# Two context attentions of 16 heads: TensorE's cycle in the order turned scores, weighted sums, scores, values, keys

## The chip, the cores and the metric

The kernel runs on one core of a Trainium2 chip. The metric is the device time of one execution in microseconds (us); lower is better. The engines are TensorE (PE in the rows; PEld is its weight load), VectorE (DVE), ScalarE (ACT), GpSimd (POOL) and the queue that issues transfers (SP).

## The reference, cut to what matters

The program is a perceiver of twelve sublayers on a residual `x` of 16 x 64 tokens of width 256, with a context of 16 x 1601 rows of width 128. Two of its sublayers, L1_xattn and L3_xattn, are context attentions with 16 heads of 16 numbers each. For each of the 16 batches and each head they compute

```
q = ln(x) @ Wq            # 64 queries
k = context @ Wk          # 1601 keys
v = context @ Wv          # 1601 values
o = softmax(q @ k.T * 0.25) @ v
x = x + o @ Wo
```

L1_xattn has biases on top of that, L3_xattn has none. All numbers are 32-bit floats. Nothing else of the program is touched by the change.

## The kernel before, in words

Both sublayers call `head_attention` (line 2740 on), the only function that changes. It walks through 16 batches of 7 units, each unit being two tiles of 128 keys (the seventh is one tile of 65). Line 2774 makes one loop of cycles `t` from -13 to 117, and every engine runs through it with its own share of the work. In cycle `t` TensorE does, for different units in a software pipeline:

- **turned scores** of unit t (`scores_turned`): four matmuls that put minus the row maximum into four PSUM banks (L2942), then 16 groups of four matmuls of keys against queries on top (L2951). ScalarE takes the exponentials of the four banks (`exps`, L3019).
- **values** of unit t+10 (`values`, L2915): one bank; VectorE copies it (`values_out`, L3095 in L3_xattn, L3098 with a bias in L1_xattn).
- **keys** of unit t+12 (`keys`, L2905): one bank; ScalarE copies it (`keys_out`, L3028).
- once a batch, **turn** (`max_turned`, L2981): the row maxima of the next batch are transposed, and VectorE makes minus_max of them (`shift_rows`, L3083).
- once a batch, **spread** (`sums_spread`, L2987): the sums of the exponentials; ScalarE copies them (L3039), VectorE inverts them and scales the output (`normal_out`, L3103 and L3105).
- in L1_xattn, in four cycles of seven, **context** (`context`, L2895): transposes of context rows into one bank, which ScalarE copies (L3047).
- **scores** of unit t+8 (`scores`, L2930): eight matmuls into four banks, from which VectorE takes maxima, one instruction for each bank (`block_max`, L3070), and after the last unit of a batch the row maximum (`row_max`, L3077).
- **weighted sums** of unit t-1 (`weighted`, L2971): 64 matmuls of exponentials against values, all into bank 7.

Below, T, V, K, C, S and W stand for turned scores, values, keys, context, scores and weighted sums. A cycle has a type, `t mod 7`: in type 5 the scores are those of the 65-key unit and the spread runs, in type 6 the turned scores are short and the turn runs, in type 0 the weighted sums are short, in type 1 the keys, in type 3 the values. Context runs in types 1 to 4 (short in type 4).

What ties the order of the work to time is the ring of PSUM banks. All fills but the weighted sums take banks 0 to 6 in turn, in TensorE's order. A fill may begin only when the fill seven places before it has been read out by its engine; `plan` (line 2803, and the loop from 2807 on) lists the fills in TensorE's order, and `wait_bank` sets the wait:

```python
if place[fill] >= banks:            # banks = 7
    by, count = taken[place[fill] - banks]
    pe.wait_ge(by.sem, by.at(count))
```

Both `scores` and `scores_turned` wait for all four of their banks before their first matmul. The order of VectorE's loop (line 3110 on) was values_out, shift_rows, block_max and row_max, normal_out; that of ScalarE's loop is exps, keys_out, sums_out, context_out, weighted_out.

Of the kernel before, what the change touches and what calls it, by code (L numbers as in the profile page):

```python
# [2739 lines left out]
def head_attention(core, room, Q, made, wv, biased, wo, wo_rows, oT, scale):  # L2740
# [16 lines left out]
    heads, d, groups = 16, 16, 4  # L2757
# [21 lines left out]
    def unit(t):  # L2779

        return divmod(t, turns) if 0 <= t < total else None

    def at_batch(t, after):

        b, rest = divmod(t - after, turns)
        return b if rest == 0 and 0 <= b < BATCH else None
# [16 lines left out]
    def plan(fill, by, count):  # L2803
        place[fill] = len(taken)
        taken.append((by, count))

    for t in cycles:
        if unit(t) is not None:
            for i in range(groups):
                plan(("turned", t, i), exp_done, 4 * t + i + 1)  # L2810
        due = []
        if unit(t + v_lead) is not None:
            due.append(("values", t + v_lead))
        if unit(t + k_lead) is not None:
            due.append(("keys", t + k_lead))
        if (b := at_batch(t, turn_at)) is not None:
            due.append(("turn", b))
        if (b := at_batch(t, spread_at)) is not None:
            due.append(("spread", b))
        if (n := context_part(t)) is not None:  # L2820
            due.append(("context", n))
        for fill in due:
            fill_no[fill] = len(fill_no)
            count, by = (dve_no, side_dve) if fill[0] in ("values", "turn") else (act_no, side_act)
            count[fill] = len(count)
            plan(fill, by, count[fill] + 1)
        if unit(t + s_lead) is not None:
            for i in range(groups):
                plan(("scores", t + s_lead, i), max_done, 4 * (t + s_lead) + i + 1)

    def bank_of(*fill):
        return place[fill] % banks
# [7 lines left out]
    with ExitStack() as own:  # L2840
# [11 lines left out]
        with nc.Block() as block:  # L2852
# [29 lines left out]
            def _(pe):  # L2882
# [36 lines left out]
                def scores(t):  # L2919
                    b, u = divmod(t + s_lead, turns)  # L2920
                    lo, cols, chunks = key_cuts(u)

                    made = act_no["keys", b * turns + u]
                    pe.wait_ge(side_act.sem, side_act.at(made + 1))
                    for i in range(groups):
                        wait_bank(pe, "scores", t + s_lead, i)
                    for n, c in enumerate(chunks):
                        for i in range(groups):
                            rows = slice(32 * i, 32 * i + 32)
                            last = nc.tensor.matmul(PS[:, bank_of("scores", t + s_lead, i), n * cols:(n + 1) * cols], Q[rows, c, b, :],  # L2930
                                                    kT[rows, b % 2, c, lo:lo + cols], start=True, stop=True)
                    last.then_inc(s_ready.sem, 1)
# [45 lines left out]
                def max_turned(b):  # L2978
                    pe.wait_ge(top_ready.sem, top_ready.at(b + 1))
                    wait_bank(pe, "turn", b)  # L2980
                    nc.tensor.transpose(PS[:, bank_of("turn", b), 0:P], M[:].rearrange("p i s -> p (i s)"),  # L2981
                                        core.ident[:]).then_inc(side_ready.sem, 1)
# [8 lines left out]
                for t in cycles:  # L2991
                    if unit(t) is not None:
                        scores_turned(t)
                    if unit(t + v_lead) is not None:
                        values(t + v_lead)
                    if unit(t + k_lead) is not None:
                        keys(t + k_lead)
                    if (b := at_batch(t, turn_at)) is not None:
                        max_turned(b)
                    if (b := at_batch(t, spread_at)) is not None:  # L3000
                        sums_spread(b)
                    if (n := context_part(t)) is not None:
                        context(n)
                    if unit(t + s_lead) is not None:
                        scores(t)
                    if unit(t - 1) is not None:
                        weighted(t - 1, 0)
                        weighted(t - 1, 1)

            @block.scalar  # L3010
            def _(act):
# [50 lines left out]
            @block.vector  # L3062
            def _(dve):
                def block_max(t):
                    b, u = divmod(t + s_lead, turns)
                    lo, cols, chunks = key_cuts(u)
                    dve.wait_ge(s_ready.sem, s_ready.at(t + s_lead + 1))
                    for i in range(groups):
                        bank = PS[:, bank_of("scores", t + s_lead, i), 0:len(chunks) * cols].rearrange("p (c s) -> p c s", s=cols)
                        nc.vector.tensor_reduce(part[:, b % 2, chunks[0]:chunks[-1] + 1, i, u // 2], bank, AX_X,  # L3070
                                                ALU.max).then_inc(max_done.sem, 1)

                def row_max(b):
                    dve.wait_ge(max_done.sem, max_done.at((b + 1) * turns * 4))
                    if b:
                        dve.wait_ge(side_ready.sem, side_ready.at(fill_no["turn", b - 1] + 1))
                    nc.vector.tensor_reduce(M[:].rearrange("p i s -> p s i")[:, 0:DC, :], part[:, b % 2], AX_X,  # L3077
                                            ALU.max).then_inc(top_ready.sem, 1)

                def shift_rows(b):  # L3080
                    dve.wait_ge(side_ready.sem, side_ready.at(fill_no["turn", b] + 1))
                    for c in range(DC):
                        last = nc.vector.tensor_scalar(shift[:, b % 2, c, :], PS[:, bank_of("turn", b), 0:P], pair_sel[:, c:c + 1], None,  # L3083
                                                       ALU.mult).then_inc(m_ready.sem, 1)
                    dve.wait_ge(m_ready.sem, m_ready.at(2 * b + 2))
                    dve.sem_inc(side_dve.sem, 1)

                def values_out(t):
                    b, j = divmod(t, turns)
                    kk, many = keys_of[2 * j], len(tiles_of(j))  # L3090
                    dve.wait_ge(side_ready.sem, side_ready.at(fill_no["values", t] + 1))
                    bank = PS[0:kk, bank_of("values", t), 0:many * DIM].rearrange("p (k h d) -> p k h d", h=heads, d=d)
                    out = V[0:kk, b % 2, 2 * j:2 * j + many, :, 0:d]
                    if not biased:
                        ins = nc.vector.tensor_copy(out, bank)  # L3095
                    else:
                        add_on = made.bv[0:kk, :].rearrange("p (h d) -> p h d", d=d).unsqueeze(1).broadcast_to([kk, many, heads, d])
                        ins = nc.vector.tensor_tensor(out, bank, add_on, ALU.add)  # L3098
                    ins.then_inc(side_dve.sem, 1)

                def normal_out(b):
                    dve.wait_ge(side_act.sem, side_act.at(act_no["spread", b] + 1))
                    nc.vector.reciprocal(inverse[:, b % 2, :], inverse[:, b % 2, :]).then_inc(inverted.sem, 1)  # L3103
                    dve.wait_ge(inverted.sem, inverted.at(b + 1))
                    nc.vector.tensor_tensor(oT[:, :, b * SEQ:(b + 1) * SEQ], O[:, b % 2, :].rearrange("p (g s) -> p g s", s=SEQ),  # L3105
                                            inverse[:, b % 2, :].rearrange("p (g s) -> p g s", s=SEQ),
                                            ALU.mult).then_inc(norm_done.sem, 1)

                nc.vector.memset(PS[:, out_bank, 0:4 * SEQ], 0.0).then_inc(filled.sem, 1)
                for t in cycles:  # L3110
                    if unit(t + v_lead) is not None:
                        values_out(t + v_lead)
                    if (b := at_batch(t, turn_at)) is not None:
                        shift_rows(b)
                    if unit(t + s_lead) is not None:
                        block_max(t)
                        if (t + s_lead) % turns == turns - 1:
                            row_max((t + s_lead) // turns)
                    if (b := at_batch(t, spread_at)) is not None:
                        normal_out(b)  # L3120
    for s in (exp_done, max_done):
# [1011 lines left out]
```

## Time and profile before

| what | us |
|---|---|
| median of 3 runs | 4622.57 |
| lowest and highest run | 4617.99, 4632.91 |
| the profiled execution's own time | 4627.87 |
| its span | 4626.1 |
| L1_xattn's loop, first to last matmul | 1668.8 to 2313.8 |
| L3_xattn's loop, first to last matmul | 3684.5 to 4288.2 |
| TensorE busy, whole span | 4177.0 (90%) |
| VectorE busy, whole span | 2563.9 (55%) |
| ScalarE busy, whole span | 1782.1 (39%) |

The two loops together are 1249 us of the span. In both, TensorE is busy for some 93 to 97 of 100 us, VectorE for 48 to 66 and ScalarE for 43 to 50. The times to read are starts of groups in the timeline: the distance from the start of one group to the start of the next is what it costs TensorE, since the ends of matmuls are modelled and overlap the next start a little.

### The profile page before, as it was taken

Reading aid. Unit: us, or ns where it says so; the run is one execution under the profiler, and the core shown is the slowest. Engines: PE = TensorE matmul, PEld = TensorE weight load, DVE = VectorE, ACT = ScalarE, POOL = GpSimd, SP = SyncE. Lnnn points to the kernel's source line nnn. Section 1 sums busy time; section 2 is a strip of 40 time slices with the busy share of each in tenths; the row PEclk is TensorE's granted clock in tenths of the full one; section 3 lists DMA queues with packets and bytes.
Section 4 is the critical chain, followed back from the end, with each engine's and each line's share of the span. In section 5 each row is a group of like instructions: output and inputs, shape, how many; then the busy total and the mean of one; then the engine's idle time right before and its main releaser. Section 6 shows DMA issues by size and latency. Waiting matters only on the chain. (4 is left out here: it accounts for less than half of the span.)

```text
span 4626.1 us, 107755 instructions
## 1 busy us (share of the span) xinstructions
PE 4177.0 (90%) x44428; PEld 3167.9 (68%) x44428; DVE 2563.9 (55%) x5138; ACT 1782.1 (39%) x3751; POOL 848.0 (18%) x556
## 2 busy tenths in 40 slices
PE   8989999999888989999976789886899999999987
PEld 5669998999667956666642379752699766666465
DVE  4468777777253055555539832246443466665454
ACT  2245555555222424444534312120254344444221
POOL 1222222221101200000029611006222100000201
PEclk9999999999988999999988899898899999999999
DMA  1010000000104821111012168649111000000100
GB/s 35 27 36 18 17 17 17 17 17 1 49 1 174 306 74 44 45 45 45 17 47 78 46 253 314 247 158 141 51 45 54 22 31 24 24 24 10 39 15 10
DMA packets 137827, 305.05 MB, mean 66 GB/s; under 512 B 51800, under 2 KB 87584, under 8 KB 119744
## 3 DMA queue, kind: packets, MB, share of 16 engines
q1 hardware_dynamic: 132992, 287.01, 19.7%
q0 software_dynamic: 4416, 12.06, 0.8%
q8 instruction: 310, 5.08, 0.5%
q14 instruction: 109, 0.89, 0.1%
HBM read 273.46 MB, written 23.47 MB: 64 GB/s over the span
## 5 line engine op out<-in xcount | busy, mean ns | idle before, releaser
L3070 DVE TENSOR_REDUCE block_max<-PS 128x1 f32<-128x512 f32 (+1 forms) x896 | 505.3, 626 | 300.7 <-PE PS L2930 299.9
L3019 ACT ACTIVATE probs_turned<-PS 128x512 f32<-128x512 f32 (+1 forms) x896 | 434.7, 570 | 562.8 <-PE PS L2951 562.7
L1149 PE MATMUL PS<-context_turned,queries 128*128 128x422 f32 (+2 forms) x1536 | 335.3, 360 | 4.8 <-ACT probs L1218 1.9
L1181 PE MATMUL PS<-probs_turned,context_part 128*128 128x256 f32 (+1 forms) x2496 | 327.7, 285 | 2.2 <-DVE weighted L1260 2.2
L1210 ACT CAST probs_turned<-PS 128x512 fp32r<-128x512 f32 (+1 forms) x512 | 232.4, 511 | 229.2 <-PE PS L1161 229.2
L1226 DVE TENSOR_TENSOR probs_turned<-PS,probs_turned 128x512 fp32r<-128x512 f32 (+1 forms) x512 | 276.5, 581 | 75.0 <-ACT probs_turned L1210 73.1
L1181 PEld LDWEIGHTS PS<-probs_turned,context_part 128*128 128x128 f32 (+1 forms) x2496 | 304.2, 189 | 2.4 <-DVE probs_turned L1226 2.4
L2971 PEld LDWEIGHTS PS<-probs_turned,values 128*17 128x17 f32 x13312 | 191.6, 97 | 150.1 <-issue 123.5
L1149 PEld LDWEIGHTS PS<-context_turned,queries 128*128 128x128 f32 x1536 | 262.5, 191 | 32.9 <-ACT probs L1218 9.0
L1218 ACT ACTIVATE probs<-PS,minus_max 128x844 f32<-128x844 f32 (+1 forms) x256 | 238.6, 932 | 105.1 <-DVE minus_max L1271 103.9
L2930 PE MATMUL PS<-keys_turned,queries 32*128 32x512 f32 (+1 forms) x2048 | 241.4, 548 | 40.9 <-ACT probs_turned L3019 35.9
L1161 PE MATMUL PS<-ident,probs 128*128 128x128 f32 (+1 forms) x1664 | 236.5, 278 | 18.5 <-DVE probs_turned L1226 16.8
L1266 DVE TENSOR_REDUCE row_max<-PS 128x1 f32<-128x844 f32 (+1 forms) x256 | 241.7, 980 | 17.7 <-issue 12.7
L2971 PE MATMUL PS<-probs_turned,values 128*17 128x64 f32 x13312 | 232.5, 220 | 10.8 <-issue 9.9
L2915 PE MATMUL PS<-L_xattn_Wv,context_turned 128*128 128x256 f32 (+1 forms) x832 | 237.3, 404 | 0.0
L134 PE MATMUL PS<-ident 128*128 128x256 f32 x706 | 199.9, 434 | 35.5 <-PEq L3940 6.9
L2951 PEld LDWEIGHTS PS<-queries,keys_turned 32*128 32x128 f32 x6656 | 221.4, 182 | 8.7 <-issue 2.3
L2951 PE MATMUL PS<-queries,keys_turned 32*128 32x128 f32 x6656 | 225.0, 270 | 0.9 <-issue 0.8
L3606 PE MATMUL PS<-prod,ident 128*128 128x512 f32 x256 | 148.9, 720 | 80.9 <-POOL prod L3541 56.4
L1161 PEld LDWEIGHTS PS<-ident,probs 128*128 128x128 f32 (+1 forms) x1664 | 185.5, 140 | 52.0 <-DVE probs_turned L1226 29.9
L2905 PE MATMUL PS<-context_turned,wk 128*128 128x512 f32 (+1 forms) x512 | 216.9, 516 | 4.5 <-POOL values L2879 3.9
L2430 PE MATMUL PS<-slot_turned,routed_up 128*128 128x128 f32 x1472 | 201.0, 278 | 4.5 <-ACT slot_turned L2360 2.6
(542 smaller groups left out, 7507.4 us busy)
## 6 DMA issues: line engine op xcount, KB each, us to landing
context_rows<-in_ctx SPq DMA_DIRECT2D x40, 768.0 KB
context_turned<-ctx_turned SPq DMA_DIRECT2D x32, 800.5 KB
routed_up<-in_L_ffn_W SPq DMA_DIRECT2D x23, 1024.0 KB, 7.9
routed_down<-in_L_ffn_W SPq DMA_DIRECT2D x23, 1024.0 KB, 6.0
routed_up<-in_L_ffn_wg_w SPq DMA_DIRECT2D x23, 1024.0 KB, 7.7
routed_second<-in_L_ffn_w_w SPq DMA_DIRECT2D x23, 1024.0 KB, 10.2
routed_down<-in_L_ffn_w_w SPq DMA_DIRECT2D x23, 1024.0 KB, 5.1
v_all<-v_turned SPq DMA_DIRECT2D x128, 128.0 KB, 17.5
```

What stands on the lines that cost most here:

```text
L1149: last = nc.tensor.matmul(PS[:, j, 0:cols], qs[a][:, v, p * P:(p + 1) * P], yT[b][:, v, at:at + cols], start=(m == 0), stop=(m == 2))
L1161: last = nc.tensor.transpose(PS[0:kk, turn_bank(it, local, j), (k - 4 * j) * P:(k - 4 * j + 1) * P], probs[:, (local - 1) % 2, k * P:k * P ...
L1181: last = nc.tensor.matmul(O_ps, yp[a][0:kk, u, k, :], probsT[b][0:kk, par, k, :], start=(k == 0 and m == 0), stop=(k == KT - 1 and m == 2))
L1218: nc.scalar.activation(out, S[half], ACT.Exp, bias=bias[:, local % 2:local % 2 + 1], scale=scale, accum_out=total[:, local, half:half + 1] ...
L1226: nc.vector.tensor_tensor(rest, bank, lead, ALU.subtract).then_inc(t_dve.sem, 1)
L1266: nc.vector.tensor_reduce(top[:, q, half:half + 1], S[half], over, ALU.max).then_inc(step.sem, 1)
L2915: last = nc.tensor.matmul(PS[0:kk, bank_of("values", t), n * DIM:(n + 1) * DIM], room.y[b % 2][:, kt * P:kt * P + kk], wv[:], start=True, ...
L2930: last = nc.tensor.matmul(PS[:, bank_of("scores", t + s_lead, i), n * cols:(n + 1) * cols], Q[rows, c, b, :], kT[rows, b % 2, c, lo:lo + c ...
L2951: last = nc.tensor.matmul(PS[0:kk, bank_of("turned", t, i), at:at + P], kT[rows, b % 2, c, kt * P:kt * P + kk], Q[rows, c, b, :], start=Fa ...
L2971: last = nc.tensor.matmul(PS[32 * i:32 * i + wide, out_bank, g * SEQ:(g + 1) * SEQ], V[0:kk, b % 2, kt, 8 * a + 4 * c + i, :], probs[0:kk, ...
L3019: nc.scalar.activation(probs[0:kk, t % ring, i, 0:many].rearrange("p k c s -> p (k c s)"), PS[0:kk, bank_of("turned", t, i), 0:many * 2 * ...
L3070: nc.vector.tensor_reduce(part[:, b % 2, chunks[0]:chunks[-1] + 1, i, u // 2], bank, AX_X, ALU.max).then_inc(max_done.sem, 1)
```

## The change

TensorE's cycle becomes T, turn, W, S, V, K, spread, C. Before it was T, V, K, turn, spread, C, S, W. `plan` lists the fills in the new order, so that the bank ring follows it. VectorE's loop becomes shift_rows, block_max and row_max, values_out, normal_out. ScalarE's loop is as before. The numbers of instructions and their shapes are the same; all leads (8, 10, 12, 13 units) are too.

```diff
     for t in cycles:
         if unit(t) is not None:
             for i in range(groups):
                 plan(("turned", t, i), exp_done, 4 * t + i + 1)
+        if (b := at_batch(t, turn_at)) is not None:
+            plan_side(("turn", b))
+        if unit(t + s_lead) is not None:
+            for i in range(groups):
+                plan(("scores", t + s_lead, i), max_done, 4 * (t + s_lead) + i + 1)
         due = []
         if unit(t + v_lead) is not None:
             due.append(("values", t + v_lead))
         if unit(t + k_lead) is not None:
             due.append(("keys", t + k_lead))
-        if (b := at_batch(t, turn_at)) is not None:
-            due.append(("turn", b))
...
-        if unit(t + s_lead) is not None:
-            for i in range(groups):
-                plan(("scores", t + s_lead, i), max_done, 4 * (t + s_lead) + i + 1)
```

```diff
                 for t in cycles:
                     if unit(t) is not None:
                         scores_turned(t)
+                    if (b := at_batch(t, turn_at)) is not None:
+                        max_turned(b)
+                    if unit(t - 1) is not None:
+                        weighted(t - 1, 0)
+                        weighted(t - 1, 1)
+                    if unit(t + s_lead) is not None:
+                        scores(t)
                     if unit(t + v_lead) is not None:
                         values(t + v_lead)
                     if unit(t + k_lead) is not None:
                         keys(t + k_lead)
-                    if (b := at_batch(t, turn_at)) is not None:
-                        max_turned(b)
...
-                    if unit(t + s_lead) is not None:
-                        scores(t)
-                    if unit(t - 1) is not None:
-                        weighted(t - 1, 0)
-                        weighted(t - 1, 1)
```

```diff
                 for t in cycles:
-                    if unit(t + v_lead) is not None:
-                        values_out(t + v_lead)
                     if (b := at_batch(t, turn_at)) is not None:
                         shift_rows(b)
                     if unit(t + s_lead) is not None:
                         block_max(t)
                         if (t + s_lead) % turns == turns - 1:
                             row_max((t + s_lead) // turns)
+                    if unit(t + v_lead) is not None:
+                        values_out(t + v_lead)
```

TensorE in L3_xattn, one whole cycle of type 2 before, from its turned scores (`minus_max`, then `queries,keys_turned`) to the next ones; values are `L_xattn_Wv,context_turned`, keys `context_turned,wk`, scores `keys_turned,queries`, weighted sums `probs_turned,values`:

```order
L2942 MATMUL PS<-minus_max,ones_wide 128x512 x4
L2951 MATMUL PS<-queries,keys_turned 128x128 x16
L2915 MATMUL PS<-L_xattn_Wv,context_turned 128x256 x2
L2905 MATMUL PS<-context_turned,wk 128x512
L2930 MATMUL PS<-keys_turned,queries 128x512 x4
L2971 MATMUL PS<-probs_turned,values 17x64 x32
L2942 MATMUL PS<-minus_max,ones_wide 128x512 x4
```

And the same place after (all line numbers of this function are 3 higher there):

```order
L2945 MATMUL PS<-minus_max,ones_wide 128x512 x4
L2954 MATMUL PS<-queries,keys_turned 128x128 x16
L2974 MATMUL PS<-probs_turned,values 17x64 x32
L2933 MATMUL PS<-keys_turned,queries 128x512 x4
L2918 MATMUL PS<-L_xattn_Wv,context_turned 128x256 x2
L2908 MATMUL PS<-context_turned,wk 128x512
L2945 MATMUL PS<-minus_max,ones_wide 128x512 x4
```

Between the turned scores and the scores stood the values and the keys, now the weighted sums; between the scores and the next turned scores stood the weighted sums, now the values and the keys.

VectorE in L3_xattn around the end of a batch before, from the maxima of the short scores (type 5) to the maxima of the next unit (type 6):

```order
L3070 TENSOR_REDUCE block_max<-PS 128x2 x4
L3077 TENSOR_REDUCE row_max<-block_max 128x2x4
L3103 RECIPROCAL row_scale<-row_scale 128x256
L3105 TENSOR_TENSOR oT<-weighted,row_scale 128x4x64
L3095 COPY values<-PS 128x32x16
L3083 TENSOR_SCALAR minus_max<-PS,pair_sel 128x128 x2
L3070 TENSOR_REDUCE block_max<-PS 128x1 x4
```

And after:

```order
L3073 TENSOR_REDUCE block_max<-PS 128x2 x4
L3080 TENSOR_REDUCE row_max<-block_max 128x2x4
L3098 COPY values<-PS 128x32x16
L3106 RECIPROCAL row_scale<-row_scale 128x256
L3108 TENSOR_TENSOR oT<-weighted,row_scale 128x4x64
L3086 TENSOR_SCALAR minus_max<-PS,pair_sel 128x128 x2
L3073 TENSOR_REDUCE block_max<-PS 128x1 x4
```

A copy of values has moved from between the scaled output and minus_max to ahead of the reciprocal; minus_max now follows the scaled output directly.

## Rows read from the trace of the kernel before

**Rows 1.** The page's section 5: the scores' group, its idle time and releasers.
```profile
L2930 PE MATMUL PS<-keys_turned,queries 32*128 32x512 f32 (+1 forms) x2048 | 241.4, 548 | 40.9 <-ACT probs_turned L3019 35.9
```

**Rows 2.** Timeline, L3_xattn, TensorE: start us, us, engine, line, out<-in xcount [idle before]
```profile
4022.55 0.50 PE L2942 MATMUL PS<-minus_max,ones_wide 32*128 32x512 f32 x4
...
4023.88 1.13 PE L2915 MATMUL PS<-L_xattn_Wv,context_turned 128*128 128x256 f32 x4
4024.84 1.02 PE L2905 MATMUL PS<-context_turned,wk 128*128 128x512 f32 x2
4025.81 1.14 PE L2930 MATMUL PS<-keys_turned,queries 32*128 32x512 f32 x8
4026.88 1.09 PE L2971 MATMUL PS<-probs_turned,values 128*17 128x64 f32 x64
4027.90 0.51 PE L2942 MATMUL PS<-minus_max,ones_wide 32*128 32x512 f32 x4
...
4031.15 1.14 PE L2930 MATMUL PS<-keys_turned,queries 32*128 32x512 f32 x8 [0.42 <-ACT probs_turned L3019]
...
4043.94 0.39 PE L2942 MATMUL PS<-minus_max,ones_wide 32*128 32x256 f32 x4
```

**Rows 3.** Timeline, L3_xattn, a cycle of type 0: TensorE, VectorE and ScalarE.
```profile
4015.19 1.14 PE L2930 MATMUL PS<-keys_turned,queries 32*128 32x512 f32 x8
...
4016.39 2.48 DVE L3070 TENSOR_REDUCE block_max<-PS 128x1 f32<-128x512 f32 x4 [1.27 <-PE PS L2930]
...
4017.23 0.51 PE L2942 MATMUL PS<-minus_max,ones_wide 32*128 32x512 f32 x4 [0.33 <-DVE block_max L3070]
...
4018.75 2.06 ACT L3019 ACTIVATE probs_turned<-PS 128x512 f32<-128x512 f32 x4 [1.41 <-PE PS L2951]
```

**Rows 4.** Timeline, L1_xattn before its first turned scores, TensorE.
```profile
1680.46 1.14 PE L2930 MATMUL PS<-keys_turned,queries 32*128 32x512 f32 x8
...
1683.70 1.14 PE L2930 MATMUL PS<-keys_turned,queries 32*128 32x512 f32 x8 [0.18 <-DVE block_max L3070]
...
1687.53 0.71 PE L2930 MATMUL PS<-keys_turned,queries 32*128 32x512 f32 x4 [0.79 <-DVE block_max L3070]
```

**Rows 5.** Timeline, L1_xattn, one batch, TensorE.
```profile
2017.86 0.39 PE L2942 MATMUL PS<-minus_max,ones_wide 32*128 32x256 f32 x4
...
2028.02 0.51 PE L2942 MATMUL PS<-minus_max,ones_wide 32*128 32x512 f32 x4 [0.33 <-DVE block_max L3070]
...
2031.75 1.14 PE L2930 MATMUL PS<-keys_turned,queries 32*128 32x512 f32 x8 [0.43 <-ACT probs_turned L3019]
...
2056.70 0.39 PE L2942 MATMUL PS<-minus_max,ones_wide 32*128 32x256 f32 x4
2056.92 0.61 PE L2951 MATMUL PS<-queries,keys_turned 32*65 32x128 f32 x16
2057.46 1.13 PE L2915 MATMUL PS<-L_xattn_Wv,context_turned 128*128 128x256 f32 x4
```

**Rows 6.** Timeline, L3_xattn, cycles of type 5 and 6: all engines.
```profile
4003.99 1.02 PE L2905 MATMUL PS<-context_turned,wk 128*128 128x512 f32 x2
...
4004.85 0.59 PE L2987 MATMUL PS<-weighted,sum_spread 128*128 128x256 f32 x2
...
4005.64 0.42 ACT L3039 COPY row_scale<-PS 128x256 f32<-128x256 f32 x1
...
4007.06 0.39 PE L2942 MATMUL PS<-minus_max,ones_wide 32*128 32x256 f32 x4
...
4007.21 1.74 DVE L3103 RECIPROCAL row_scale<-row_scale 128x256 f32<-128x256 f32 x1
...
4008.98 0.42 DVE L3105 TENSOR_TENSOR oT<-weighted,row_scale 128x256 f32<-128x256 f32 x1
...
4009.96 0.61 DVE L3083 TENSOR_SCALAR minus_max<-PS,pair_sel 128x128 fp32r<-128x128 f32 x2
```

**Rows 7.** Busy time by stretch, us and count: PE PEld DVE ACT POOL, granted clock, DMA share, GB/s.
```profile
2200.00:2300.00 100.00, 92.77 (x2223) 64.81 (x2220) 55.70 (x99) 50.38 (x111) 0.00 (x0) 1.00 0.05 19
```

More of the change, by code:

```diff
@@ L2805, in plan, with plan_side @@
         taken.append((by, count))
+    def plan_side(fill):
+        fill_no[fill] = len(fill_no)
+        count, by = (dve_no, side_dve) if fill[0] in ("values", "turn") else (act_no, side_act)
+        count[fill] = len(count)
+        plan(fill, by, count[fill] + 1)
     for t in cycles:
@@ L2822, in head_attention @@
         for fill in due:
[L2823 to L2826, printed above, removed]
-        if unit(t + s_lead) is not None:
-            for i in range(groups):
-                plan(("scores", t + s_lead, i), max_done, 4 * (t + s_lead) + i + 1)
+            plan_side(fill)
     def bank_of(*fill):
```

## The prediction

> **What bounds the kernel now.** I read the page's groups first. Only the two 16-head attentions change, so their groups matter: the scores (S) have TensorE idle for 40.9 us ahead of them over both, 35.9 us of it until ScalarE has read turned scores [rows 1]. That is the wait which this order of work touches, and it is no more than 0.8% of the kernel.
>
> Next comes the timeline of TensorE in the steady part, because only the distances between starts say what a step costs. A full cycle of L3_xattn is T 1.33 (4023.88 - 4022.55), V 0.96, K 0.97, S 1.07, W 1.02, in all 5.35, and none of it is a wait [rows 2]. TensorE is the bound here. In the next cycle V is short and S waits 0.42 for ScalarE: it starts 3.25 after T [rows 2]. The wait is for a bank. The ring has seven banks; with V and K between T and S, the last scores bank is the one that the third turned bank left. With one fill more between (context, in L1_xattn) it is the fourth, and S starts 3.73 after T [rows 5]. So exponentials come free 0.48 apart: fourth 3.73, third 3.25, and by the same step second 2.76 and first 2.27 after T (the last two are estimates from these rows).
>
> VectorE has its own staircase. The maxima start 1.20 after S and take 2.48 for four [rows 3]. Where the next waiting fill needs only the first of them read, it starts 2.04 after S (4017.23 - 4015.19) [rows 3]. Where it needs three, or four, the part of L1_xattn before its first turned scores shows it: there a cycle is S, V, K, and the next S starts 3.24 later, idle 0.18 for block_max; with a context fill between as well it starts 3.83 later, idle 0.79 in spite of the extra work [rows 4]. One step is 0.6, so first 2.04, third 3.24 and fourth 3.83 agree.
>
> **The change, part by part.** No instruction is added or removed. What moves is the distance, in fills and in time, between a bank's fill and its next use.
>
> *The wait of S.* Between T and S now stands W, which takes no bank, so the last scores bank needs only the first exponential read, 2.27 after T. TensorE gets there at 1.33 + 1.02 = 2.35 [rows 2]. The wait is gone in the full cycles, and 0.08 is all the cover that is left. In type 0 W is half as long, TensorE is there at about 1.9, and S starts at 2.27.
>
> *The wait of T.* Before, between S and the next T stood W alone, with no fill, and T needed one maximum: 2.04 after S, where TensorE came at 1.07 + 1.02 = 2.09 (hidden, but in type 0). Now V and K stand between, two fills, and T's fourth bank is the one of the third score: 3.24 after S. TensorE comes at 1.07 + 0.96 + 0.97 = 3.00. So T waits 0.24 in a full cycle, and where V or K is short it waits longer and the short fill gains nothing. Everything behind T on TensorE's queue waits with it. In L1_xattn with context three fills stand between, and T needs all four maxima: 3.83.
>
> So a cycle of types 1 to 4 costs 2.35 + 3.24 = 5.59 in L3_xattn and 2.35 + 3.83 = 6.18 in L1_xattn. Type 0 costs 2.27 + 3.24 = 5.51. Type 5 has the short scores, whose maxima are done early, and the spread: T 1.33, W 1.02, S some 0.60, V 0.96, K 0.86 and spread 0.59 [rows 2, 6], about 5.37, the same work as before with no wait.
>
> *The order on VectorE, type 5 into 6.* Before, the spread ran ahead of the short scores and its reciprocal began right after row_max. Now the spread comes last in the cycle. Count from the start of S in type 5: the next T is at 5.37 - 2.35 = 3.02, the spread at 2.43, K at 1.57; ScalarE's copy starts 1.65 after K (4005.64 - 4003.99) and takes 0.42, so it ends at 3.64; the reciprocal runs from 3.7, the product 1.77 later at 5.47, until 5.89; then minus_max 0.61, to 6.50 [rows 6]. The maxima of the next scores stand behind that. Without it they would start at 3.02 + 0.76 + 0.2 + 1.02 + 1.20 = 6.20 (short T 0.76 [rows 5]; the turn's 0.2 is an estimate, a third of the spread), so they are 0.3 late. The third maximum releases T 3.24 - 1.20 = 2.04 after they begin, at 8.54: type 6 costs 8.54 - 3.02 = 5.52. If nothing were late it would be 5.22.
>
> *The sum of a batch.* L3_xattn: 5.51 + 4 x 5.59 + 5.37 + 5.52 = 38.76, against 4043.94 - 4007.06 = 36.88 [rows 2, 6]: 1.88 more. L1_xattn: 5.51 + 4 x 6.18 + 5.37 + 5.52 = 41.12, against 2056.70 - 2017.86 = 38.84 [rows 5]: 2.28 more. K runs out at t = 99 of 112, so cycles 1 to 98 are 14 full batches: 26.3 and 31.9, together **58.2 us**.
>
> *Edges.* Before the first turned scores the order S, V, K is the old one turned round, with the same waits; the first S comes one V and K earlier (-1.9), and the first T waits for three maxima in place of one (+1.2): -0.7 in each stage. The first batch has no reciprocal (-0.3 each). In the last cycles V or K is missing, and what a shorter wait of S gives, T's wait takes back: 0, between -1 and +1. In all about -2.
>
> *What costs nothing.* W needs exponentials of the cycle before, a cycle old now as then. weighted_out (ScalarE, behind keys_out) ends some 0.2 before the next W wants bank 7. Copies of values start 3.7 after S and end by 4.5, a microsecond before the next S needs their bank. SP's transfers of context hang on V, K or context of a batch, each later by under a cycle, with more than ten cycles to land in. ScalarE's order is unchanged and it is busy half the time [rows 7].
>
> The sum is +56. On the profiled execution's 4627.87 that is 4684; that one is 5.3 above the median of the three runs, so for the median I take 4622.6 + 56 = **4679 us**.
>
> **A rule against the order, weighed.** In a stretch of L1_xattn in which TensorE waited about as often as it will now, it was busy for 92.77 of 100 us and the granted clock stayed 1.00, the 2.4 GHz level [rows 7]. The Trainium skill, Perfetto Trace Analysis, section Matmul Optimizations, says that TensorE's power follows its use, so that matmuls should run back to back. By that rule a gap in every cycle could cost clock on top of the gap. By rows 7 the sum has no term for it; the rule's result is the third rival.
>
> **The rivals.**
>
> *Faster: the wait of T is not there.* VectorE would have to finish three maxima in 3.00 after S rather than 3.24; the point is a maximum of 0.52 rather than 0.60. Then only the gain is left, at most all of the 35.9 us for which S waited on ScalarE [rows 1]: 4587. For it speaks that the gap is only 0.24, under a tenth of a microsecond per instruction. Against it speaks that rows 4 show this very wait, behind the same V and K. 4 in 100.
>
> *A smaller cost.* If T in a context cycle had only to wait for three maxima, TensorE's own work would set it, at some 5.8 rather than 6.18: 0.4 x 56 cycles = 22 less, 4657; a reciprocal that delays nobody gives 0.3 x 26 = 8 less, 4671. The fourth bank follows from counting fills, and rows 4 show 3.83. 6 in 100 for the first.
>
> *The clock falls.* If one twentieth of the two stages (1249 us in all) ran at 1.2 GHz, the same work would take double there: about +60, 4739. 3 in 100, since rows 7 show no such fall.
>
> *S waits for a later exponential.* The cover is 0.08. If the first exponential came 0.1 to 0.18 later after T than I take it, each of 140 cycles (types 1 to 5, 14 batches, both stages) would lose 0.02 to 0.1: 3 to 14 more, up to 4693, inside my range. If it were the second (2.76), each would lose 0.4 and type 0 0.5: 0.4 x 168 = 67 more, 4746. 3 in 100.
>
> That the change does not do what it says is excluded by the order of the built program: V and K stand where W stood.
>
> **How the numbers follow.** The forecast, T held by VectorE in both stages, has 84 in 100. The range goes from 4655, the smaller cost, to 4705: 4679, plus 14 for the uncovered exponential, plus 10 for runs that spread over 15 us before. It leaves out the clock, the second exponential, the faster rival and some tails, about 13 to 18 in 100. A difference of under 0.3%, 14 us, is about what a measurement can't tell from none. Faster by more than that: 4 in 100, the first rival. Within: 2 in 100, a mix of the two signs. Slower: 94 in 100.
>
> **What would show it.** In the profile after: the idle time before the turned scores (L2945) rises from a few us to some 60 to 90, with block_max as its releaser; that before the scores (L2933) falls to a few us. T to T is 5.59 in L3_xattn and 6.18 in the context cycles of L1_xattn, S to T 3.24 and 3.83, the half-length values or keys no longer shorten a cycle, and type 6 is near 5.5. The maxima behind the reciprocal begin at once after minus_max. I am wrong if T starts 3.00 after S with no wait, if S still waits for ScalarE in full cycles, or if the granted clock falls in these stages.

## The result and the profile after

The changed kernel takes 4683.61 us (median of 3 runs, 4682.37 to 4683.94), against 4622.57 before: a ratio of 1.0119, 95% interval 1.0091 to 1.0147. It is 61 us slower by the medians; the profiled execution has 4683.61 us as well (span 4681.7), 55.7 more than the 4627.87 of the profiled one before. The forecast was +56 on the profiled execution and 4679 for the median.

The page's groups show the exchange of one wait for another. The first line below is the turned scores' group of the kernel before, the others are of the page and of the groups by line of the kernel after (line, engine, operation, count, then busy us, mean ns, then idle us before it with its releasers):

```profile
L2942 PE MATMUL PS<-minus_max,ones_wide 32*128 32x512 f32 (+1 forms) x896 | 109.6, 477 | 15.2 <-DVE block_max L3070 12.8 <-DVE minus_max L3083 1.1 <-issue 0.7
```

```profile
span 4681.7 us, 107756 instructions
L2933 PE MATMUL PS<-keys_turned,queries 32*128 32x512 f32 (+1 forms) x2048 | 244.1, 550 | 16.2 <-ACT probs_turned L3022 9.8
L2945 PE MATMUL PS<-minus_max,ones_wide 32*128 32x512 f32 (+1 forms) x896 | 110.4, 472 | 84.9 <-DVE block_max L3073 81.7 <-DVE minus_max L3086 2.1 <-ACT probs_turned L3022 0.6
```

TensorE's idle time ahead of the scores fell from 40.9 us [rows 1] to 16.2, and ahead of the turned scores it rose from 15.2 to 84.9, of which 81.7 ended with a maximum of VectorE. The two changes together are 45 us; idle time shows less than the starts do, since the modelled end of the last matmul covers a part of each wait.

The timeline of TensorE in L3_xattn, from a full cycle (type 2) and the one with short values (type 3) on to the short turned scores (type 6) of this batch and of the next, answers to [rows 2, 3]. The first line is the short turned scores of the batch before:

```profile
4014.93 0.39 PE L2945 MATMUL PS<-minus_max,ones_wide 32*128 32x256 f32 x4
...
4031.48 0.51 PE L2945 MATMUL PS<-minus_max,ones_wide 32*128 32x512 f32 x4 [0.65 <-DVE block_max L3073]
...
4032.81 1.09 PE L2974 MATMUL PS<-probs_turned,values 128*17 128x64 f32 x64
4033.83 1.14 PE L2933 MATMUL PS<-keys_turned,queries 32*128 32x512 f32 x8
4034.90 1.13 PE L2918 MATMUL PS<-L_xattn_Wv,context_turned 128*128 128x256 f32 x4
4035.87 1.02 PE L2908 MATMUL PS<-context_turned,wk 128*128 128x512 f32 x2
4037.07 0.51 PE L2945 MATMUL PS<-minus_max,ones_wide 32*128 32x512 f32 x4 [0.18 <-DVE block_max L3073]
...
4042.66 0.51 PE L2945 MATMUL PS<-minus_max,ones_wide 32*128 32x512 f32 x4 [0.67 <-DVE block_max L3073]
...
4048.24 0.50 PE L2945 MATMUL PS<-minus_max,ones_wide 32*128 32x512 f32 x4 [0.18 <-DVE block_max L3073]
...
4053.54 0.39 PE L2945 MATMUL PS<-minus_max,ones_wide 32*128 32x256 f32 x4
...
4059.02 0.50 PE L2945 MATMUL PS<-minus_max,ones_wide 32*128 32x512 f32 x4 [0.39 <-DVE block_max L3073]
...
4064.52 0.51 PE L2945 MATMUL PS<-minus_max,ones_wide 32*128 32x512 f32 x4 [0.17 <-DVE block_max L3073]
...
4092.37 0.39 PE L2945 MATMUL PS<-minus_max,ones_wide 32*128 32x256 f32 x4
```

T to T is 5.59 (4037.07 - 4031.48), and 5.59 again where the values are short: what the short fill saves is added to the wait (0.67 in place of 0.18). S starts 2.35 after T with no wait, and T comes 3.24 after S. A batch is 38.61 (4053.54 - 4014.93), as most of them are; the next is 38.83, with a pause of 0.2 in it. In a full cycle T starts 0.24 later than TensorE's own work would have it, where the idle time shows 0.18. The same for L1_xattn, with one of its cycles that have a context fill, between the short turned scores of two batches, which answers to [rows 5]:

```profile
1990.52 0.39 PE L2945 MATMUL PS<-minus_max,ones_wide 32*128 32x256 f32 x4
...
2007.68 0.50 PE L2945 MATMUL PS<-minus_max,ones_wide 32*128 32x512 f32 x4 [0.80 <-DVE block_max L3073]
...
2010.02 1.14 PE L2933 MATMUL PS<-keys_turned,queries 32*128 32x512 f32 x8
...
2013.86 0.51 PE L2945 MATMUL PS<-minus_max,ones_wide 32*128 32x512 f32 x4 [0.34 <-DVE block_max L3073]
...
2031.52 0.39 PE L2945 MATMUL PS<-minus_max,ones_wide 32*128 32x256 f32 x4
```

Here T is 3.84 after S, the cycle is 6.18, and the batch is 41.00 (2031.52 - 1990.52). Other batches of this stage take up to 1.9 us more (before, up to 2.9 us more than 38.84); over 13 batches these extras come to some 10 us in both kernels, and what they are was not followed.

By stage: L1_xattn's loop, from its first matmul to its last, took 645.0 us before and takes 675.3 (1667.3 to 2342.6, +30.3); L3_xattn's took 603.7 and takes 627.4 (3717.1 to 4344.5, +23.7). Together that is 54.0 of the 55.6 us by which the span grew.

### The profile page after: what moved, and what is told of

It is laid out like the page before. It is cut to its first block and busy times, and to the rows that moved or that the text cites. A ratio compares the mean times of both kernels' runs of the same rounds, so it can differ in the third digit from the quotient of the medians.

```text
span 4681.7 us, 107756 instructions
## 1 busy us (share of the span) xinstructions
PE 4185.3 (89%) x44428; PEld 3167.9 (68%) x44428; DVE 2548.0 (54%) x5138; ACT 1797.9 (38%) x3751; POOL 848.1 (18%) x556
## 5 line engine op out<-in xcount | busy, mean ns | idle before, releaser
L3031 ACT ACTIVATE keys_turned<-PS 128x512 f32<-128x512 f32 (+1 forms) x256 | 125.7, 504 | 421.1 <-PE PS L2908 421.1
L2933 PE MATMUL PS<-keys_turned,queries 32*128 32x512 f32 (+1 forms) x2048 | 244.1, 550 | 16.2 <-ACT probs_turned L3022 9.8
L2918 PEld LDWEIGHTS PS<-L_xattn_Wv,context_turned 128*128 128x128 f32 (+1 forms) x832 | 137.0, 185 | 157.7 <-issue 141.8
## 6 DMA issues: line engine op xcount, KB each, us to landing
v_all<-v_turned SPq DMA_DIRECT2D x128, 128.0 KB, 18.5
```

The costliest lines, as they stand in the source:

```text
L2918: last = nc.tensor.matmul(PS[0:kk, bank_of("values", t), n * DIM:(n + 1) * DIM], room.y[b % 2][:, kt * P:kt * P + kk], wv[:], start=True, ...
```

## Experiments

All times are medians; a ratio is to the kernel before measured beside it on the same chip, whose own median was 4629.32 us there for half_after, half_before, values_first and late_reciprocal, and 4624.83 for the other four. The expectations count from 4684 and 4623, so a few us of a median's distance from its expectation can be this; the profiled spans (4626.1 before, 4681.7 after) are compared beside it.

**Half of the maxima's work, changed order (half_after).** Each `block_max` reads the first half of its columns; the maxima over the other half are left out.

```diff
-bank = PS[:, bank_of("scores", t + s_lead, i), 0:len(chunks) * cols].rearrange("p (c s) -> p c s", s=cols)
+bank = PS[:, bank_of("scores", t + s_lead, i), 0:len(chunks) * cols].rearrange("p (c s) -> p c s", s=cols)[:, :, 0:cols // 2]
```

> The changed order, with each block_max read over the first half of the keys of its bank only (so the row maxima come from half of the keys; the softmax is shifted by another number, everything else is computed as before). Theory, VectorE's maxima hold the turned scores: a maximum over half as many numbers steps 0.33 us rather than 0.60, so the third is read 2.44 and the fourth 2.76 after the start of the scores, before TensorE has done values and keys (3.00). The wait is gone, a full cycle is 5.35, short values or keys shorten it to about 4.9, and the batch is about 36.1 in L3_xattn and 37.3 in L1_xattn, against 38.8 and 41.0 in the profile after: 4592 us. Rival, the time went into TensorE's own order (weighted sums between others, or the clock): no change, 4684.

Measured: 4577.84 us, ratio 0.9887 (0.9871 to 0.9902). The new order is now faster than the kernel before. Groups by line, and the timeline of a cycle with short values and the full one behind it in L3_xattn:

```profile
L2945 PE MATMUL PS<-minus_max,ones_wide 32*128 32x512 f32 (+1 forms) x896 | 109.3, 478 | 4.9 <-DVE block_max L3073 2.1 <-DVE minus_max L3086 2.0 <-ACT probs_turned L3022 0.6
```

```profile
3993.46 0.50 PE L2945 MATMUL PS<-minus_max,ones_wide 32*128 32x512 f32 x4
...
3998.31 0.50 PE L2945 MATMUL PS<-minus_max,ones_wide 32*128 32x512 f32 x4
...
4003.64 0.50 PE L2945 MATMUL PS<-minus_max,ones_wide 32*128 32x512 f32 x4
```

The wait of T has gone from 84.9 us to 4.9, the cycle with short values is 4.85 (3998.31 - 3993.46) and the full one 5.33 (4003.64 - 3998.31). A batch is 35.97 in L3_xattn and 37.34 in L1_xattn (36.1 and 37.3 expected). The four maxima take 1.42 us rather than 2.48. The cause is VectorE's staircase of maxima. The profiled span is 96.5 us below that of the kernel after, where 92 was expected; the median lies another 9 below the profiled execution, inside the spread of its runs (4574.71 to 4587.03).

**The same cut, order of before (half_before).** The same edit.

> The order of before with the same half maxima (row maxima from half of the keys). Theory: there the turned scores wait for the first maximum only, in type 0, and that comes 0.27 earlier: 28 x 0.27 = 8 us, and some 3 us in the first cycles, 4612 us; the waits of the scores for ScalarE stay. Rival, VectorE's load holds both orders alike: the same gain as in the changed order, 4530.

Measured: 4611.36 us, ratio 0.9960 (0.9947 to 0.9972). A cut that gives the new order about 100 us gives the old one some 18 by the medians and 12.7 by the profiled spans (4613.4 against 4626.1), where 11 were expected: a batch is 36.60 rather than 36.88 in L3_xattn and 38.58 rather than 38.84 in L1_xattn, 7.6 us over 14 batches each. VectorE's load as such holds neither; the place of the maxima in the ring decides. With this cut in both, the new order is the faster one (4577.84 against 4611.36): its weighted sums hide most of the wait for ScalarE (idle ahead of the scores 11.1 us against 35.9), and the wait for VectorE is gone.

**The ring one bank shorter, changed order (six_banks).**

```diff
-    ring, banks, out_bank = 3, 7, 7
+    ring, banks, out_bank = 3, 6, 7
```

> The changed order with a ring of six banks instead of seven, nothing else. Theory: every fill waits for the one six before it. S needs the second exponential (2.76 after T, was 2.35 by TensorE's work), T needs the fourth maximum (3.83 after S, was 3.24) and with context the copy of values behind the maxima (about 4.5). A full cycle of L3_xattn is 6.59, of L1_xattn with context about 7.3: about 180 us more, 4860. Rival, what T waits for is VectorE being late with its whole work and not a place in the ring: no change, 4684.

Measured: 4860.91 us, ratio 1.0512 (1.0491 to 1.0533). Timeline of TensorE, L3_xattn, one full cycle:

```profile
4114.98 0.50 PE L2945 MATMUL PS<-minus_max,ones_wide 32*128 32x512 f32 x4 [1.24 <-DVE block_max L3073]
...
4117.73 1.14 PE L2933 MATMUL PS<-keys_turned,queries 32*128 32x512 f32 x8 [0.34 <-ACT probs_turned L3022]
...
4121.56 0.51 PE L2945 MATMUL PS<-minus_max,ones_wide 32*128 32x512 f32 x4 [0.77 <-DVE block_max L3073]
```

S comes 2.75 after T, the second exponential (2.76 by the steps), and T comes 3.83 after S, the fourth maximum. Both waits have moved up by exactly one step, with no work added. In L1_xattn's cycles with context T came 4.43 after S, and 4.16 where the values are short, released by the copy of values (about 4.5 expected). The wait is one for a place in the ring.

**Values between T and S, keys between W and T (values_first).** TensorE: T, turn, V, S, W, K, spread, C, with `plan` to match; VectorE: minus_max, values, maxima, normal.

```diff
                         max_turned(b)
-                    if unit(t - 1) is not None:
-                        weighted(t - 1, 0)
-                        weighted(t - 1, 1)
+                    if unit(t + v_lead) is not None:
+                        values(t + v_lead)
                     if unit(t + s_lead) is not None:
                         scores(t)
-                    if unit(t + v_lead) is not None:
-                        values(t + v_lead)
+                    if unit(t - 1) is not None:
+                        weighted(t - 1, 0)
+                        weighted(t - 1, 1)
```

> Cycle T, turn, V, S, W, K, spread, C with VectorE in the order minus_max, values, maxima, normal. One fill stands between T and S and one (two with context) between S and the next T. Theory, fills times steps: S starts when the second exponential is read, 2.76 after T, and T needs two maxima, 2.64 after S, so TensorE's S, W and K (3.06) set it: full cycle 5.82, type 0 and 1 about 5.4 in L3_xattn; batches of about 39.1 and 40.7, 4679 us. Rival, the waits have nothing to do with the place in the ring: S starts 2.29 after T with no wait and a full cycle is 5.35, 4620.

Measured: 4699.43 us, ratio 1.0144 (1.0126 to 1.0162): slower than the kernel before, and 20 us more than expected. By the profiled spans it is also slower than the kernel after, by 18.5 us (4700.2 against 4681.7); the intervals of the two ratios overlap. Timeline of L3_xattn, first TensorE, then VectorE in the type 6 of the same batch:

```profile
4048.60 0.50 PE L2945 MATMUL PS<-minus_max,ones_wide 32*128 32x512 f32 x4
...
4051.36 1.14 PE L2933 MATMUL PS<-keys_turned,queries 32*128 32x512 f32 x8 [0.31 <-ACT probs_turned L3022]
...
4054.51 0.51 PE L2945 MATMUL PS<-minus_max,ones_wide 32*128 32x512 f32 x4
...
4060.38 0.39 PE L2945 MATMUL PS<-minus_max,ones_wide 32*128 32x256 f32 x4
...
4062.41 1.14 PE L2933 MATMUL PS<-keys_turned,queries 32*128 32x512 f32 x8
...
4065.86 0.51 PE L2945 MATMUL PS<-minus_max,ones_wide 32*128 32x512 f32 x4 [0.24 <-DVE block_max L3073]
...
4100.34 0.39 PE L2945 MATMUL PS<-minus_max,ones_wide 32*128 32x256 f32 x4
```

```profile
4063.82 0.69 DVE L3098 COPY values<-PS 128x512 f32<-128x512 f32 x1
4064.43 2.48 DVE L3073 TENSOR_REDUCE block_max<-PS 128x1 f32<-128x512 f32 x4
```

S starts 2.76 after T, as the steps say (the second exponential, one fill between). The miss lies elsewhere: S to T is 3.15 rather than 3.06, since K costs 1.06 in front of T (it starts at 4053.45) where 0.97 was taken; and in type 6 the maxima stood behind the reciprocal and product of the batch, minus_max and the values copy, one directly after the other from 4060.94 on, started 2.0 after S instead of 1.20, and made that type 5.48 (4065.86 - 4060.38) rather than 5.04. A batch of L3_xattn is 39.96 (4100.34 - 4060.38) rather than 39.07.

**VectorE's loop alone as before (old_vector_order).** TensorE in the changed order; `values_out` ahead of minus_max and the maxima on VectorE.

```diff
                 for t in cycles:
+                    if unit(t + v_lead) is not None:
+                        values_out(t + v_lead)
                     if (b := at_batch(t, turn_at)) is not None:
                         shift_rows(b)
...
-                    if unit(t + v_lead) is not None:
-                        values_out(t + v_lead)
```

> TensorE in the changed order, VectorE's loop in the order of before (values_out ahead of minus_max and the maxima). Theory: the copy of values, which TensorE now makes after the scores, stands ahead of the maxima on VectorE; they start 2.95 after S rather than 1.20, and T waits 1.7 more in every cycle but type 5: about 320 us more, 5000. Rival, VectorE's order doesn't matter since it is busy half the time: 4684.

Measured: 5115.43 us, ratio 1.1062 (1.1038 to 1.1087), some 115 more than expected. Busy times of two stretches (PE PEld DVE ACT POOL, granted clock, DMA share, GB/s), and the timeline of TensorE in L3_xattn:

```profile
1720.00:2400.00 680.00, 515.49 (x9489) 348.18 (x9492) 276.28 (x488) 241.74 (x517) 0.00 (x0) 0.91 0.09 31
3900.00:4600.00 700.00, 530.53 (x9305) 346.79 (x9309) 309.26 (x564) 230.65 (x480) 2.01 (x4) 0.92 0.07 21
```

```profile
4198.89 0.51 PE L2945 MATMUL PS<-minus_max,ones_wide 32*128 32x512 f32 x4 [1.81 <-DVE block_max L3073]
...
4200.22 1.91 PE L2974 MATMUL PS<-probs_turned,values 128*17 128x64 f32 x64
4202.06 1.92 PE L2933 MATMUL PS<-keys_turned,queries 32*128 32x512 f32 x8
...
4206.95 0.50 PE L2945 MATMUL PS<-minus_max,ones_wide 32*128 32x512 f32 x4 [1.54 <-DVE block_max L3073]
...
4214.16 0.51 PE L2945 MATMUL PS<-minus_max,ones_wide 32*128 32x512 f32 x4 [1.81 <-DVE block_max L3073]
...
4251.92 0.50 PE L2945 MATMUL PS<-minus_max,ones_wide 32*128 32x512 f32 x4 [1.81 <-DVE block_max L3073]
...
4258.38 0.50 PE L2945 MATMUL PS<-minus_max,ones_wide 32*128 32x512 f32 x4 [1.54 <-DVE block_max L3073]
```

A full cycle is 7.21 (4214.16 - 4206.95), close to the theory's 5.59 + 1.7 = 7.29. What it left out is the clock: at 4200 the weighted sums and the scores take 1.9 us each, nearly twice the 1.09 and 1.14 of [rows 2], that is the 1.2 GHz level. The cycle with short values that begins at 4198.89 takes 8.06 for it; the one of the next batch, all at the 2.4 GHz level, takes 6.46 (4258.38 - 4251.92). Two estimates say what this costs in all. A mean of 0.91 to 0.92 means that about 17% of the stretches ran at half the rate; if TensorE's own work had set the time throughout, that would be half of 0.17 x 1380 us, about 117 us. And in L3_xattn the cycles of each type that ran at the 2.4 GHz level add up to about 48.6 us a batch, where 14 batches took 736.9: some 56 us more in this stage, and by the same reckoning some 50 in L1_xattn. By the profiled spans the miss is 110 us (5108.0 - 4681.7 = 426, 316 expected), so the clock accounts for about all of it.

**The reciprocal one cycle later (late_reciprocal).** VectorE's `normal_out` behind the maxima and values of type 6; the loop runs one cycle longer for the last of them.

```diff
-    cycles = range(-c_lead, total + 6)
+    cycles = range(-c_lead, total + 7)
...
-                    if (b := at_batch(t, spread_at)) is not None:
+                    if (b := at_batch(t, spread_at + 1)) is not None:
                         normal_out(b)
```

> The changed order, with normal_out (reciprocal and product) one cycle later on VectorE, behind the maxima of type 6. Theory: the maxima of type 6 start 0.3 earlier and type 6 goes from 5.48 to 5.22: 26 x 0.26 = 7 us less, 4677. Rival, the reciprocal then ends late for the maxima of type 0 and what is gained comes back: 4684.

Measured: 4677.86 us (4668.46 to 4682.06), ratio 1.0104 (1.0087 to 1.0120). Timeline of L3_xattn, TensorE: type 6 is 4054.01 - 4048.73 = 5.28, and type 0 behind it keeps its 5.49, so that nothing is handed back.

```profile
4048.73 0.39 PE L2945 MATMUL PS<-minus_max,ones_wide 32*128 32x256 f32 x4
...
4054.01 0.50 PE L2945 MATMUL PS<-minus_max,ones_wide 32*128 32x512 f32 x4 [0.18 <-DVE block_max L3073]
...
4059.50 0.51 PE L2945 MATMUL PS<-minus_max,ones_wide 32*128 32x512 f32 x4 [0.17 <-DVE block_max L3073]
```

So type 6 gives back 0.20 rather than the 0.26 expected, since the turn costs TensorE 0.06 more than was taken (see the part on why the prediction was right). The profiled spans differ by 6.5 us (4675.2 against 4681.7), where 7 was expected, but only 4.3 of it lie between the first and the last T of the two stages; the rest is elsewhere in the program, where nothing was changed. The medians (4677.86 and 4683.61) differ by less than those of the kernel before that were measured beside them (4629.32 and 4622.57), so that only the timeline carries this one.

**Waits bank by bank, changed order (bank_by_bank_after).** T and S wait for each bank ahead of its own matmul. The edit in `scores_turned`, and the one in `scores`:

```diff
-                    for i in range(groups):
-                        wait_bank(pe, "turned", t, i)
                     many = len(tiles_of(j))
                     for i in range(groups):
+                        wait_bank(pe, "turned", t, i)
```

```diff
-                    for i in range(groups):
-                        wait_bank(pe, "scores", t + s_lead, i)
                     for n, c in enumerate(chunks):
                         for i in range(groups):
+                            if n == 0:
+                                wait_bank(pe, "scores", t + s_lead, i)
```

> The changed order, in which T and S wait for each of their four banks just ahead of the matmul that needs it, not for all four ahead of the first. Theory: three of the four minus_max matmuls run while the last waits; the 0.31 from the first of them to the keys-against-queries matmuls shrinks to about 0.1, so 0.2 less in each of six cycle types: 28 x 6 x 0.2 = 34 less, 4650. Rival, the group's end is set by its last bank however it starts: 4684.

Measured: 4650.85 us, ratio 1.0050 (1.0031 to 1.0069), against 1.0119 without it. Part of each wait is now under the first three matmuls, and what is left of it stands inside the group, so that it is counted as busy time:

```profile
L2944 PE MATMUL PS<-minus_max,ones_wide 32*128 32x512 f32 (+1 forms) x896 | 179.0, 480 | 10.2 <-DVE minus_max L3085 2.3 <-DVE block_max L3072 0.4
```

The total agrees better than its term. A batch went from 38.61 to 37.84 in L3_xattn and from 41.00 to 40.23 in L1_xattn: 0.77 each, where the theory has 6 x 0.2 = 1.2. That is 22 us over 14 batches each. The span fell by 30.4 (4651.3 against 4681.7), since L1_xattn's batches had fewer pauses in this execution (some 5 us), and the rest came from elsewhere.

**Waits bank by bank, order of before (bank_by_bank_before).** The same edit.

> The order of before with the same waits bank by bank. Theory: S waits 0.4 in five cycle types of fourteen and T 0.33 in two; of each wait 0.1 to 0.2 is hidden: 7 to 14 less, 4612. Rival, nothing is hidden: 4623.

Measured: 4605.16 us, ratio 0.9959 (0.9946 to 0.9971). This computes everything and beats both kernels. Timeline of L3_xattn, the cycle with short keys:

```profile
4038.62 1.46 PE L2930 MATMUL PS<-keys_turned,queries 32*128 32x512 f32 x8
4040.01 1.09 PE L2970 MATMUL PS<-probs_turned,values 128*17 128x64 f32 x64
```

The scores start without a wait and take 1.39 to the next start rather than 1.07: of a wait of some 0.4 ahead of them [rows 2], 0.32 are still there, now inside the group, and 0.1 is hidden. In type 0, T starts 1.64 after S rather than 2.04; together with the cycle behind it this gives 0.24. A batch is 36.44 rather than 36.88 in L3_xattn and 38.25 rather than 38.84 in L1_xattn, and 14 batches of both stages take 14.4 us less, the upper end of what was expected. The medians differ by 19.7 and the profiled spans by 23.7 (4602.4 against 4626.1): another 4 come from the last cycles of the stages, and the rest from outside of them.

## Why the prediction was right

**The order is bound by a loop through the ring, and that was the step that decided.** T fills four banks, ScalarE reads them, S needs one of them, VectorE reads S's banks, T needs one of those. How many reads each side waits for is the number of fills in between. The forecast took both staircases from waits that the kernel before already showed [rows 2 to 5] and moved along them; the first and second exponential were estimates there, and type 0 after (2.26) and six_banks (2.75) measure them. The trace after has the values:

| term | forecast | profile after |
|---|---|---|
| T to S, full cycle, no wait | 2.35 | 2.35 |
| T to S, type 0, first exponential | 2.27 | 2.26 |
| S to T, third maximum | 3.24 | 3.24 |
| S to T, fourth maximum | 3.83 | 3.84 |
| type 0 | 5.51 | 5.50 |
| types 1 to 4, L3_xattn | 5.59 | 5.58 to 5.60 |
| types 1 to 4, L1_xattn | 6.18 | 6.18 |
| type 5 | 5.37 | 5.30 |
| type 6 | 5.52 | 5.48 |
| a batch of L3_xattn | 38.76 | 38.61 |
| a batch of L1_xattn | 41.12 | 41.00 |
| profiled time | +56 | +55.7 |

**The wait of S** went as said: 2.35 after T in full cycles, the cover of 0.08 held. That leaves 16.2 us of idle time before the scores, more than the few us I named, since S in type 0 waits 0.30 for the first exponential 28 times, some 8 us; the sum had that time, the sentence on the idle row did not. Most of the rest was there before too: 5.0 of the 40.9 us had nothing to do with turned scores [rows 1].

**The wait of T** is the cost: 84.9 us of idle time, inside the 60 to 90 of the forecast. It started from 15.2, not from the few us that the forecast names. half_after removes it, six_banks moves it by one step.

**The order on VectorE in types 5 and 6** was right in its mechanism and 0.04 high in its size, and that small error is what is left of larger ones. These are rows of TensorE and VectorE after, in L3_xattn:

```profile
4050.59 0.68 PE L2933 MATMUL PS<-keys_turned,queries 32*128 32x65 f32 x16
...
4053.02 0.59 PE L2990 MATMUL PS<-weighted,sum_spread 128*128 128x256 f32 x2
...
4054.11 1.75 DVE L3106 RECIPROCAL row_scale<-row_scale 128x256 f32<-128x256 f32 x1 [1.06 <-ACT row_scale L3042]
...
4056.24 0.60 DVE L3086 TENSOR_SCALAR minus_max<-PS,pair_sel 128x128 fp32r<-128x128 f32 x2
...
4056.99 2.48 DVE L3073 TENSOR_REDUCE block_max<-PS 128x1 f32<-128x512 f32 x4
```

The short scores began at 4050.59, so the reciprocal began 3.52 after them (3.7 in the forecast) and the maxima 6.40 after (6.50). minus_max follows the reciprocal's chain at once and the maxima follow minus_max. The chain began 0.18 earlier than forecast and took 0.08 longer (2.88 from the start of the reciprocal to that of the maxima, 2.80 in the forecast). Without the chain type 6 is 5.28, as late_reciprocal shows, and not 5.22: the turn costs TensorE 0.26, where 0.2 was the estimate. So the delay is 0.20 rather than 0.3.

**Type 5** came out 0.07 cheaper than the old one: its spread costs 0.52 in front of T (4053.54 - 4053.02), where I had 0.59.

**The 14 batches and the edges.** These are starts of T in the two timelines, at cycle 1 and at cycle 99:

| stage | before | after | difference of the lengths |
|---|---|---|---|
| L1_xattn | 1712.21, 2265.08 | 1709.66, 2292.49 | 582.83 - 552.87 = 29.96 |
| L3_xattn | 3722.60, 4238.92 | 3756.19, 4296.61 | 540.42 - 516.32 = 24.10 |

The 98 cycles cost 54.1 us, where the forecast has 58.2: a batch costs 1.73 more in L3_xattn (1.88 forecast) and 2.16 more in L1_xattn (2.28), mostly by types 5 and 6, and the first batch a little less. The two stages as a whole grew by 54.0, so the edges came to nothing where the forecast has -2. The span grew by 1.6 outside of the stages. So a miss of 4 us in the batches was made good by 2 at the edges and 1.6 outside: that the profiled time came to within 0.3 us of +56 is luck, while the batches themselves are within 4 of 58 us of the forecast.

**The rivals.** *Faster, no wait of T:* the point it named, a shorter maximum, is what half_after makes, and there the new order is 1.1% faster than the kernel before and 0.7% faster than the kernel before with the same cut; with full maxima the wait is there. *Smaller cost:* excluded, T is 3.84 after S in context cycles. *Clock:* in the profile after, the granted clock is 1.00 in L1_xattn from 1720 to 2290 us and in L3_xattn from 3720 to 4344. It did not fall there, where T waits 0.2 to 0.8; it fell in old_vector_order, where T waits 1.5 to 2.6, so a loss of clock behind longer waits is real, and this change does not reach it. The Trainium skill, Perfetto Trace Analysis, section Matmul Optimizations, says that matmuls should run back to back because the engine's power follows its use. The trace of the kernel after shows no cost of that kind at its gaps (granted clock 1.00); that of old_vector_order shows one, about 117 us by the estimate above. *A later exponential:* excluded in full cycles by the missing wait.

## What to carry to other kernels

In a ring of buffers, moving work from one side of a fill to the other changes which read the next fill waits for, not only when it is issued: count the fills between, multiply by the reader's step, and compare with the work that covers it. Here each fill moved from between T and S to between S and T exchanges a step of ScalarE (0.49 us) for one of VectorE (0.60). In L3_xattn the loop through the ring was 3.25 + 2.04 = 5.29 before, just under the 5.35 of TensorE's own work, and is 2.27 + 3.24 = 5.51 after, 5.59 with the weighted sums that end at 2.35: 0.22 us of steps were enough to change what bounds the cycle. The steps can be read off any stretch of the old trace in which the same wait is already exposed, often at a stage's start; and where one wait for four buffers stood ahead of four instructions, it was cheaper here in both orders to let each wait for its own.

## What was not expected of the hardware

In old_vector_order the granted clock fell to 0.91 and 0.92 of full over the two stages, with T waiting 1.5 to 2.6 us in its cycles; in six_banks, with two waits in a cycle, of 0.3 to 0.8 us for S and of 0.8 to 1.4 us for T, it stayed at the 2.4 GHz level in the two stretches below, though TensorE was busy only 80% of the time there:

```profile
1720.00:2320.00 600.00, 482.73 (x9798) 326.04 (x9786) 283.94 (x505) 248.66 (x531) 0.00 (x0) 1.00 0.11 36
3900.00:4500.00 600.00, 486.62 (x10327) 323.32 (x10314) 302.93 (x538) 242.47 (x513) 0.00 (x0) 1.00 0.06 19
```

What separates the two is left open; no run varies the length of one wait alone.
